# Turning normalised tokens with VectorE block transposes and SBUF-to-SBUF DMAs in a four-layer hybrid kernel

## The chip, the core and the metric

The kernel runs on one core of one Trainium2 chip. The time is device microseconds of one execution; the median of three runs of the kernel before is 2016.64 us.

## What is computed

The input x is 8 sequences of 1024 tokens with 256 features, float32. Four layers follow each other, each with a layernorm (no scale, no shift) in front and a residual around it:

```
x = x + softmax_attention(layernorm(x))   # 2 heads of 128, causal, half of each head rotated
x = x + feed_forward(layernorm(x))        # 768 hidden: (silu(x wg) * (x wu)) wd, integer weights / 127
x = x + linear_attention(layernorm(x))    # 8 heads of 64, elu+1 features, per-head decay, tanh gate
x = x + feed_forward(layernorm(x))        # the same weights again
```

The matrices multiply float32 values as a high part and a low part (`F32R`), in two to four matmuls each.

## The kernel before, in words

X, all 8192 tokens, stays in SBUF for the whole kernel: 64 tiles of 128 tokens by 256 features. The work goes in units of 512 tokens (UT = 4 tiles): 16 units per layer. Every projection needs the normalised tokens the other way round, features on the partitions, so each unit passes through the same steps, always for the unit or batch that comes next:

- VectorE (DVE) takes statistics (L121) and aggregates (L129), GpSimd (POOL) takes the reciprocal root (L153, L156), DVE normalises into `ln_xn` (L141).
- `SplitTransposed.pe` (L181 to L188) turns the unit on TensorE (PE): 8 transposes of 128x128 (4 tiles, 2 feature groups) into two PSUM banks.
- `act` (L192) copies the 128x1024 result out of PSUM as the high part, on ScalarE (ACT).
- `dve` (L196) subtracts it from the PSUM copy and writes the low part. `pe_wait` lets PE go on to the projections.

Each engine has its own list of instructions, written out by hand and run in order; semaphores (`Signal`) tie them together. An instruction that waits holds back everything behind it on its engine.

**Softmax attention** (`attention_phase`, L243): a turn per batch of 1024 tokens. First 8 query/key projections and the value projections, then 16 steps n (token tile i = n // 2, head n % 2), each with scores, row maximum, exponential, transposed probabilities, weighted values and output projection. In step 4 and 6 DVE takes the statistics of the next batch, in 9 and 11 it normalises, and in steps 14 and 15 PE, ACT and DVE turn and split the two halves. SP loads X in a loop (L333), one batch behind another, all before 52 us. POOL adds the rotated parts.

**Feed-forward** (`feed_forward_phase`, L722): a turn per unit, six iterations f. PE's order in each is gate(f), up(f), down(f-2); ACT's is silu(f), high part of h(f-1) (L818, L811); DVE's is h(f) (L865), low part of h(f-1) (L845), and at f = 1 the residual of the unit before (L852). Statistics are at f = 0 and 2, the normalisation at 3, PE's transposes at 4 (after up, before down), ACT's copy at the end of 4, DVE's subtraction at the start of 5. The parts have two sets of buffers, for even and odd units. SP only stores the output in the second feed-forward (L781).

**Linear attention** (`linear_attention_phase`, L955): a turn per batch, two halves of 512 tokens. 16 projections with their activations, then four chunks c: scores, outputs, state, keys; the gated output goes through a high part on ACT (`gated_high`) and a low part on POOL (`gated_low`). Statistics lie among the projections, the normalisation before chunk 0 (L1266), the transposes and the split in chunk 3 (L1422, L1147, L1273). The parts have one set of buffers.

## Time and profile before

| | |
|---|---|
| runs | 2016.64 us median, 2015.66 to 2017.07 |
| the profiled execution | span of 2018.8 us from the first to the last instruction, the one time there is for it |
| granted TensorE clock | 0.990 of 2.4 GHz over the span |
| PE / DVE / ACT / POOL busy | 1942.5 / 1340.9 / 890.8 / 335.7 us |
| softmax attention, feed-forward, linear attention, feed-forward | about 0 to 566, 569 to 858, 873 to 1720, 1726 to 2019 us |

Busy time is the sum of an engine's instructions; PE's matmuls overlap, and their ends are modelled, so starts are read rather than ends. A wait is shown in square brackets: the idle time before an instruction and what ended it. A line number is that of the kernel before; `SPq` and `ACTq` are the engines' queues issuing DMAs.

### The profile page before, as it was taken

What the parts mean: (1) busy time and instruction counts of PE and PEld (TensorE: products, weight loads), DVE (VectorE), ACT (ScalarE), POOL (GpSimd) and SP (SyncE); (2) the same over time, 40 slices, a digit from 0 to 9 for tenths busy, and PEclk for the clock granted to TensorE, in tenths of its full rate; (3) what the DMA queues carried; (4) which work ended last, traced back from release to release, by engine and by line L of the source; (5) the groups of instructions that cost most, each with busy time, mean ns of one, the idle gap of its engine ahead of it and who ended that gap; (6) DMA issues with size and microseconds to landing.
All of it is one profiled execution on the core that took longest, in us unless ns stands there. A gap on an engine that the chain in (4) does not pass through costs nothing. (4 is left out here: it accounts for less than half of the span.)

```text
span 2018.8 us, 36941 instructions
## 1 busy us (share of the span) xinstructions
PE 1942.5 (96%) x12803; PEld 1678.0 (83%) x12803; DVE 1340.9 (66%) x3222; ACT 890.8 (44%) x1708; POOL 335.7 (17%) x314
## 2 busy tenths in 40 slices
PE   6999999999899999979999999999999999999998
PEld 5888888888688888858888888888888888788887
DVE  5666566656557777756666666666666666677776
ACT  4556555655554444453333333333333333444443
POOL 2112211221100000032222222221222112000000
PEclk9999999999999999989999999999999999899999
DMA  6100000000010000010000000000000000000000
GB/s 221 48 1 0 0 0 0 0 0 0 1 53 0 0 0 0 0 52 1 2 1 1 0 0 0 0 0 0 0 0 0 0 1 1 11 32 31 31 29 34
DMA packets 21983, 27.91 MB, mean 14 GB/s; under 512 B 1057, under 2 KB 20129, under 8 KB 21537
## 3 DMA queue, kind: packets, MB, share of 16 engines
q1 hardware_dynamic: 20800, 24.32, 3.6%
q10 hardware_dynamic: 1120, 2.75, 0.4%
q8 instruction: 39, 0.64, 0.1%
q14 instruction: 24, 0.19, 0.0%
HBM read 18.69 MB, written 8.39 MB: 13 GB/s over the span
## 5 line engine op out<-in xcount | busy, mean ns | idle before, releaser
L818 ACT ACTIVATE ff_silu<-PS 128x512 f32<-128x512 f32 x192 | 115.3, 600 | 290.1 <-PE PS L903 290.1
L865 DVE SCALAR_TENSOR_TENSOR ff_h<-PS,ff_silu 128x512 f32<-128x512 f32 x192 | 132.8, 692 | 125.0 <-PE PS L903 114.0
L1119 ACT ACTIVATE lin_yg_hi<-stage 128x512 fp32r<-128x512 f32 x64 | 40.4, 632 | 384.9 <-DVE stage L1234 373.3
L914 PE MATMUL PS<-ff_w_hi,ff_h_hi 128*128 128x256 f32 x768 | 193.7, 285 | 1.0 <-ACT ff_h_hi L811 1.0
L914 PE MATMUL PS<-ff_w_hi,ff_h_lo 128*128 128x256 f32 x768 | 191.9, 282 | 0.0
L1084 POOL TENSOR_TENSOR lin_yg_lo<-stage,lin_yg_hi 128x512 fp32r<-128x512 f32 x64 | 81.9, 1280 | 577.6 <-ACT lin_yg_hi L1119 577.6
L1196 DVE TENSOR_TENSOR lin_AD<-PS,lin_decay 128x512 f32<-128x512 f32 x128 | 82.1, 682 | 131.5 <-PE PS L1342 131.5
L227 PE MATMUL PS<-ln_xh,lin_w_hi 128*128 128x512 f32 x384 | 152.4, 397 | 15.0 <-DVE lin_w_lo L1165 15.0
L903 PE MATMUL PS<-ln_xh,ff_w_hi 128*128 128x512 f32 x384 | 153.9, 401 | 5.1 <-ACT ff_w_hi L806 2.7
L633 PE MATMUL PS<-probT,v_a 128*128 128x128 f32 x1152 | 154.0, 279 | 4.1 <-DVE oT_lo L495 4.1
L633 PEld LDWEIGHTS PS<-probT,v_a 128*128 128x128 f32 x1152 | 138.9, 192 | 19.3 <-issue 12.7
L914 PEld LDWEIGHTS PS<-ff_w_hi,ff_h_hi 128*128 128x128 f32 x768 | 145.6, 190 | 10.8 <-ACT ff_h_hi L811 1.4
L903 PE MATMUL PS<-ln_xl,ff_w_hi 128*128 128x512 f32 x384 | 153.8, 401 | 0.0
L227 PE MATMUL PS<-ln_xl,lin_w_hi 128*128 128x512 f32 x384 | 151.0, 393 | 0.0
L227 PE MATMUL PS<-ln_xh,lin_w_lo 128*128 128x512 f32 x384 | 150.9, 393 | 0.0
L903 PE MATMUL PS<-ff_odd_xl,ff_w_hi 128*128 128x512 f32 x384 | 150.8, 393 | 0.0
L903 PE MATMUL PS<-ff_odd_xh,ff_w_hi 128*128 128x512 f32 x384 | 150.4, 392 | 0.0
L914 PEld LDWEIGHTS PS<-ff_w_hi,ff_h_lo 128*128 128x128 f32 x768 | 146.3, 190 | 4.9
L605 PE MATMUL PS<-qk 128*128 128x512 f32 (+3 forms) x384 | 144.7, 488 | 0.0
L500 DVE TENSOR_REDUCE neg_max<-PS 128x1 f32<-128x256 f32 (+7 forms) x128 | 96.6, 755 | 67.2 <-PE PS L608 65.6
L1355 PE MATMUL PS<-lin_v,lin_AD 128*128 128x65 f32 x1024 | 133.3, 273 | 0.0
L153 POOL TENSOR_SCALAR ln_var_eps<-ln_mean_var 128x4 f32<-128x4 f32 (+1 forms) x56 | 13.0, 231 | 718.3 <-DVE ln_mean_var L129 718.3
(156 smaller groups left out, 4934.2 us busy)
## 6 DMA issues: line engine op xcount, KB each, us to landing
X<-in_x SPq DMA_DIRECT2D x8, 1024.0 KB, 5.3
out_x<-X SPq DMA_DIRECT2D x16, 512.0 KB, 2.9
stage<-in_w_lin SPq DMA_DIRECT2D x1, 2048.0 KB, 7.6
stage<-in_w_gate SPq DMA_DIRECT2D x2, 768.0 KB, 4.3
stage<-in_w_up SPq DMA_DIRECT2D x2, 768.0 KB, 5.8
stage<-in_w_down SPq DMA_DIRECT2D x2, 768.0 KB, 8.1
cos<-in_cos ACTq DMA_DIRECT2D x1, 1024.0 KB, 8.3
qk<-in_w_qkv ACTq DMA_DIRECT2D x1, 768.0 KB, 7.2
```

What stands on the lines that cost most here:

```text
L227: last = nc.tensor.matmul(out, w, x, start=n == 0, stop=n == len(terms) - 1)
L500: nc.vector.tensor_reduce(neg_max[:, n:n + 1], score_rows(n), AX.X, ALU.max, negate=True).then_inc(max_done.sem, 1)
L605: last = nc.tensor.matmul(bank[:, 0:w], qk[:, 0, h, i * P:(i + 1) * P], qk[:, 1, h, c:c + w], start=True, stop=not diag)
L633: last = nc.tensor.matmul(O, V[:, j, h * DA:(h + 1) * DA], probT[:, n % 2, j, :], start=j == 0, stop=j == i)
L818: nc.scalar.activation(silu[:, f % 2, :], PS[:, 2 + f % 2, :], ACT.Silu, scale=W_SCALE).then_inc(silu_done.sem, 1)
L865: nc.vector.scalar_tensor_tensor(h[:, f % 2, :], PS[:, 4 + f % 2, :], W_SCALE, silu[:, f % 2, :], ALU.mult, ALU.mult).then_inc(h_done.sem, 1)
L903: ins = nc.tensor.matmul(PS[:, bank, :], w, x, start=n == 0, stop=n == len(parts) - 1)
L914: ins = nc.tensor.matmul(Y[:, t // 2, (t % 2) * M:(t % 2 + 1) * M], a[:, f % NH, t * P:(t + 1) * P], w[:, f % NF, :], start=f == 0 and n = ...
L1084: nc.gpsimd.tensor_tensor(yg_lo[:], yg, yg_hi[:].bitcast(F32), ALU.subtract).then_inc(yg_lo_done.sem, 1)
L1119: nc.scalar.activation(yg_hi[:], yg, ACT.Copy).then_inc(yg_hi_done.sem, 1)
L1196: nc.vector.tensor_tensor(AD[:, c % 2, r], PS[:, r, :].rearrange("p (j t) -> p j t", t=P), D[:].rearrange("p (j r) t -> p r j t", r=2)[:, ...
L1355: last = nc.tensor.matmul(bank[:, hh * VA:(hh + 1) * VA], AD[:, ch % 2, hh % 2, 2 * g + hh // 2, :], v[:, c, HG * g + hh, :], start=hh == ...
```

## The change

The transposes on PE go, in all four layers, and `SplitTransposed` with them. A unit is now turned so:

- DVE writes the normalised tokens with their features in four groups of 32, so that each group's columns of a unit stand together (`by_feature_group`).
- DVE transposes every 32x32 block of the unit in one instruction (`dve_blocks`).
- SP moves the blocks to their places with 16 DMAs inside SBUF, for each of four row groups and four column groups: 32 partitions by 8 pieces of 32 floats, 32 KB (`sp_move`). They land in the buffer of the low part.
- ACT copies that buffer as the high part (`act_high`), POOL subtracts it in place (`pool_low`). Neither touches PSUM.

In the softmax attention the block buffer is `swapped`, so SP waits until the values of the batch are projected, and the statistics, normalisations and blocks stand at steps 2, 4, 6 to 9 and ACT's copies at 11 and 13; SP loads batch 0 and 1 first and batch b + 2 in turn b. In the feed-forwards the statistics are taken a unit earlier, at f = 4 and 5, the normalisation is at f = 0, the blocks at f = 1, ACT's copy ahead of silu(4). In the linear attention SP waits for the half's last projection, and ACT's copy comes before the first `gated_high`. In the second feed-forward each store stands on SP behind the moves of a unit.

```diff
+SQ = 32
+NQ = P // SQ
+MOVES = NQ * NQ
+def by_feature_group(buf, t):
+    return buf.rearrange("p t m -> p (t m)").rearrange("p (c k t b) -> p c k t b", c=NQ, k=KT, t=UT)[:, :, :, t, :]
...
-            last = nc.vector.tensor_scalar(self.out[:, t, :], self.X[:, bass.ds(turn * self.tiles + t, 1), :],
-                                           self.mean_var[:, t, 0:1], self.rstd[:, t:t + 1],
+            out = by_feature_group(self.out[:, t // UT * UT:(t // UT + 1) * UT, :], t % UT)
+            x = self.X[:, bass.ds(turn * self.tiles + t, 1), :].rearrange("p a (k c b) -> p c (a k) b", k=KT, b=SQ)
+            last = nc.vector.tensor_scalar(out, x, self.mean_var[:, t, 0:1], self.rstd[:, t:t + 1],
...
+    def dve_blocks(self, dve, unit, before=None):
+        dve.wait_ge(self.ln.ready.sem, self.ln.ready.at(unit, self.unit + 1))
+        if before:
+            front, n = before
+            dve.wait_ge(front.landed.sem, front.landed.at(n, 16 * MOVES))
+        self.nc.vector.transpose(self.blocks.rearrange("p t m -> p (t m)"),
+                                 self.ln.out[:, self.unit * UT:(self.unit + 1) * UT, :].rearrange("p t m -> p (t m)")).then_inc(self.blocks_done.sem, 1)
+    def sp_move(self, sp, unit, par):
+        wait_alone(sp, self.blocks_done.sem, self.blocks_done.at(unit, 1), self.sp_passed)
+        lo = self.parts[par][1][:].bitcast(F32)
+        for r in range(NQ):
+            for c in range(NQ):
+                src = self.blocks[r * SQ:(r + 1) * SQ, c, :].rearrange("p (n b) -> p n b", b=SQ)
+                dst = lo[c * SQ:(c + 1) * SQ].rearrange("p k (t r b) -> p (k t) r b", t=UT, r=NQ)[:, :, r, :]
+                sp.dma_start(dst, src).then_inc(self.landed.sem, 16)
+    def act_high(self, act, unit, par):
+        hi, lo = self.parts[par]
+        act.wait_ge(self.landed.sem, self.landed.at(unit, 16 * MOVES))
+        self.nc.scalar.activation(hi[:], lo[:].bitcast(F32), ACT.Copy).then_inc(self.hi_done.sem, 1)
+    def pool_low(self, pool, unit, par):
+        hi, lo = self.parts[par]
+        pool.wait_ge(self.hi_done.sem, self.hi_done.at(unit, 1))
+        self.nc.gpsimd.tensor_tensor(lo[:], lo[:].bitcast(F32), hi[:].bitcast(F32),
+                                     ALU.subtract).then_inc(self.lo_done.sem, 1)
...
+        odd = sb("a1_xh", [P, KT, UN], F32R), sb("a1_xl", [P, KT, UN], F32R)
+        turned = [Turned(nc, ctx, f"a{half}", ln, swapped[:, 2 * half:2 * half + 2, :].rearrange("p s (z m) -> p (s z) m", m=M),
+                         env["norm"].parts if half == 0 else odd, half) for half in range(NHALF)]
+        sx = [t.pair(0) for t in turned]
...
+                def load_x(b):
+                    at = bass.ds(b * TB, TB)
+                    sp.dma_start(X[:, at, :], x_v[:, at, :]).then_inc(x_loaded, 16)
+                load_x(0)
+                for t in turned:
+                    t.sp_open(sp)
+                following.sp_open(sp)
                 sp.wait_ge(w_loaded, 16)
-                sp.wait_ge(x_loaded, 16)
-                with sp.Fori(0, NB - 1) as p:
-                    at = bass.ds((p + 1) * TB, TB)
-                    sp.dma_start(X[:, at, :], x_v[:, at, :]).then_inc(x_loaded, 16)
-                    wait_alone(sp, x_loaded, (p + 2) * 16, passed)
-
+                for t in turned:
+                    t.sp_move(sp, 0, 0)
+                load_x(1)
+                def turn(b, more):
+                    if more:
+                        wait_alone(sp, x_loaded, b * 16 + 32, passed)
+                        load_x(b + 2)
+                    wait_alone(sp, v_ready.sem, v_ready.at(b, TB), passed)
+                    for t in turned:
+                        t.sp_move(sp, b + 1, 0)
+                with sp.Fori(0, NB - 2) as b:
+                    turn(b, True)
                 load_ff_weights(sp, env, io)
+                turn(NB - 2, False)
+                sp.wait_ge(v_ready.sem, v_ready.at(NB - 1, TB))
+                following.sp_move(sp, 0, 0)
...
-                        if n >= NS - NHALF and not last:
-                            sx[n - (NS - NHALF)].act(act, b + 1)
-                        if n == NS - 2 and last and following:
-                            following.sx.act(act, 0)
+                        if n in (11, 13) and not last:
+                            turned[(n - 11) // 2].act_high(act, b + 1, 0)
+                        if n == NS - 3 and last:
+                            following.act_high(act, 0, 0)
...
-                        elif not last:
-                            sx[n + 2 - NS].dve(dve, b + 1)
-                        elif n + 2 == NS and following:
-                            following.sx.dve(dve, 0)
...
-                            if n in (4, 6):
+                            if n in (2, 4):
                                 dve.wait_ge(x_loaded, (b + 2) * 16)
-                                ln.dve_tile_stats(dve, b + 1, range(0, UT) if n == 4 else range(UT, TB))
-                            if n == 6:
+                                ln.dve_tile_stats(dve, b + 1, range(0, UT) if n == 2 else range(UT, TB))
+                            if n == 4:
                                 ln.dve_aggregate(dve, b + 1)
-                            if n in (9, 11):
-                                ln.dve_normalise(dve, b + 1, range(0, UT) if n == 9 else range(UT, TB))
-                        if n == 7 and last and following:
+                            if n in (6, 8):
+                                ln.dve_normalise(dve, b + 1, range(0, UT) if n == 6 else range(UT, TB))
+                            if n in (7, 9):
+                                if n == 7:
+                                    dve.wait_ge(rotated.sem, rotated.at(b, 2 * NHALF))
+                                turned[(n - 7) // 2].dve_blocks(dve, b + 1)
+                        if n == 6 and last:
                             following.ln.dve_normalise(dve, 0)
+                        if n == 7 and last:
+                            following.dve_blocks(dve, 0)
...
-                        if n + 2 >= NS and not last:
-                            sx[n + 2 - NS].pe(pe, b + 1, b + 1)
-                        if n + 2 == NS and last and following:
-                            following.sx.pe(pe, 0, 0)
...
+                def unit(u, par, first, left):
+                    upcoming = next_of(u, par, left)
+                    if upcoming:
+                        nfront, nu, npar = upcoming
+                        if not first:
+                            wait_alone(sp, up_ready.sem, up_ready.at(u - 1, NF), front.sp_passed)
+                        nfront.sp_move(sp, nu, npar)
+                    if following and first:
+                        sp.wait_ge(prep_lo, NPART)
+                        load_lin_weights(sp, env, io)
+                    if not following and not first:
+                        store(u - 1)
+                def store(u):
+                    wait_alone(sp, x_done.sem, x_done.at(u, 1), front.sp_passed)
+                    at = bass.ds(u * UT, UT)
+                    sp.dma_start(out_v[:, at, :], X[:, at, :]).then_inc(stored, 16)
...
+                def unit(u, par, first, left):
+                    upcoming = next_of(u, par, left)
+                    if upcoming:
+                        nfront, nu, npar = upcoming
+                        nfront.pool_low(pool, nu, npar)
+                    after = after_next(u, left)
+                    if after:
+                        after[0].pool_rstd(pool, after[1])
...
+                        if f == NF - 2 and upcoming:
+                            nfront, nu, npar = upcoming
+                            nfront.act_high(act, nu, npar)
                         act.wait_ge(gate_ready.sem, gate_ready.at(u, f + 1))
                         act.wait_ge(h_done.sem, h_done.at(u, f - 1))
                         nc.scalar.activation(silu[:, f % 2, :], PS[:, 2 + f % 2, :], ACT.Silu,
                                              scale=W_SCALE).then_inc(silu_done.sem, 1)
                         if f > 0 or not first:
                             high_part(u, f - 1)
-                        if f == NF - 2 and upcoming:
-                            _, _, nsx, nturn = upcoming
-                            nsx.act(act, nturn)
...
-                        if f == NF - 1 and upcoming:
-                            nsx.dve(dve, nturn)
...
-                        if f == 3 and upcoming:
-                            nln.dve_normalise(dve, nln_turn)
...
-                            if f == 0:
-                                nln.dve_tile_stats(dve, nln_turn, range(0, UT // 2))
-                            if f == 2:
-                                nln.dve_tile_stats(dve, nln_turn, range(UT // 2, UT))
-                                nln.dve_aggregate(dve, nln_turn)
-                    if last:
+                        if upcoming and f == 0:
+                            upcoming[0].ln.dve_normalise(dve, upcoming[1])
+                        if upcoming and f == 1:
+                            upcoming[0].dve_blocks(dve, upcoming[1], (front, u))
+                        if after and f == NF - 2:
+                            after[0].dve_tile_stats(dve, after[1], range(UT))
+                        if after and f == NF - 1:
+                            after[0].dve_aggregate(dve, after[1])
...
-                            if f == NF - 2 and upcoming:
-                                _, nln_turn, nsx, nturn = upcoming
-                                nsx.pe(pe, nturn, nln_turn)
...
+                def turn(b, first, last):
+                    for half in range(NHALF):
+                        nfront, n = next_of(b, half, last)
+                        wait_alone(sp, proj_ready.sem, proj_ready.at(b, NITEM * (half + 1)), front.sp_passed)
+                        nfront.sp_move(sp, n, 0)
...
+                            if c == 0:
+                                nfront.pool_low(pool, n, 0)
...
+                            if c == 0:
+                                nfront, n = next_of(b, half, last)
+                                nfront.act_high(act, n, 0)
...
+                        nfront.dve_blocks(dve, nturn, (front, b * NHALF + half))
...
-                            elif upcoming:
-                                pe.wait_ge(ad_done.sem, ad_done.at(b, 2 * ch + 2))
-                                upcoming[1].pe(pe, upcoming[2], upcoming[2])
```

## Rows read from the trace of the kernel before

**Rows 1.** The page: span, busy time of the engines, and DMA queue q1.
```profile
span 2018.8 us, 36941 instructions
...
PE 1942.5 (96%) x12803; PEld 1678.0 (83%) x12803; DVE 1340.9 (66%) x3222; ACT 890.8 (44%) x1708; POOL 335.7 (17%) x314
...
q1 hardware_dynamic: 20800, 24.32, 3.6%
```

**Rows 2.** Busy time by stage: the softmax attention from 20 to 566 us (window, its length, busy us).
```profile
20.00:566.00 546.00, 528.44 (x3513) 443.13 (x3513) 335.92 (x807) 320.07 (x789) 100.61 (x81) 1.00 0.05 15
```

**Rows 3.** Groups of instructions: name, count, busy us, mean ns of one, idle before and releaser.
```profile
L186 PE MATMUL PS<-ident,ln_xn 128*128 128x128 f32 x512 | 69.7, 281 | 14.1 <-DVE ln_xn L141 14.1
...
L192 ACT ACTIVATE ln_xh<-PS 128x1024 fp32r<-128x1024 f32 x40 | 41.2, 1029 | 18.5 <-PE PS L186 18.5
...
L196 DVE TENSOR_TENSOR ln_xl<-PS,ln_xh 128x1024 fp32r<-128x1024 f32 x40 | 49.0, 1225 | 37.6 <-ACT ln_xh L192 37.6
...
L1079 POOL TENSOR_TENSOR lin_w_o_lo<-stage,lin_w_o_hi 128x1024 fp32r<-128x1024 f32 x1 | 2.4, 2352 | 0.0
...
L156 POOL TENSOR_TENSOR ln_rstd<-ln_var_eps,ln_minus_half 128x4 f32<-128x4 f32 (+1 forms) x56 | 63.2, 1128 | 4.7
```

**Rows 4.** Timeline of DVE in one feed-forward unit (start, length in us): h(0) twice.
```profile
702.17 0.69 DVE L865 SCALAR_TENSOR_TENSOR ff_h<-PS,ff_silu 128x512 f32<-128x512 f32 x1 [0.38 <-PE PS L903]
...
719.99 0.69 DVE L865 SCALAR_TENSOR_TENSOR ff_h<-PS,ff_silu 128x512 f32<-128x512 f32 x1 [0.38 <-PE PS L903]
```

**Rows 5.** SP's DMA issues in order of time, and the time from issue to landing of one.
```profile
860.58 0.34 SPq L1040 DMA_DIRECT2D lin_bias<-in_b_g  x1
...
860.97 1.30 SPq L1041 DMA_DIRECT2D lin_decay_in<-in_decay  x1
...
862.32 0.43 SPq L1042 DMA_DIRECT2D lin_AD<-in_dist  x1
...
862.78 0.43 SPq L1043 DMA_DIRECT2D lin_rev<-in_rev  x1
...
lin_AD<-in_dist SPq DMA_DIRECT2D x1, 192.0 KB, 2.4
```

**Rows 6.** Timeline of DVE and ACT in the same feed-forward unit.
```profile
703.38 0.74 DVE L121 BATCH_NORM_STATS2 ln_stats<-X 128x6 f32 x2
...
704.05 0.60 ACT L818 ACTIVATE ff_silu<-PS 128x512 f32<-128x512 f32 x1 [1.68 <-PE PS L903]
```

**Rows 7.** PE's first matmul of the feed-forward, and two windows (the number before DMA's is PEclk).
```profile
568.81 0.77 PE L903 MATMUL PS<-ln_xh,ff_w_hi 128*128 128x512 f32 x1 [2.42 <-issue]
...
568.10:574.90 6.80, 6.09 (x14) 4.79 (x15) 1.18 (x3) 6.08 (x7) 0.00 (x0) 0.50 0.32 92
...
1726.50:1732.00 5.50, 5.48 (x13) 4.34 (x14) 5.50 (x5) 4.39 (x4) 0.00 (x0) 0.50 0.00 0
```

**Rows 8.** Timeline of one half of the linear attention: ACT, DVE, PE.
```profile
1226.72 0.63 ACT L1119 ACTIVATE lin_yg_hi<-stage 128x512 fp32r<-128x512 f32 x1 [11.50 <-DVE stage L1234]
...
1215.70 1.29 DVE L1196 TENSOR_TENSOR lin_AD<-PS,lin_decay 128x512 f32<-128x512 f32 x2 [3.98 <-PE PS L1342]
...
1232.79 1.04 PE L186 MATMUL PS<-ident,ln_xn 128*128 128x128 f32 x8
...
1233.66 1.00 PE L1355 MATMUL PS<-lin_v,lin_AD 128*128 128x65 f32 x8
```

**Rows 9.** Timeline of one batch of the softmax attention: steps 7, 11 and 13.
```profile
258.06 0.47 DVE L513 SCALAR_TENSOR_TENSOR X<-PS,row_inv,X 128x256 f32 x1
...
271.25 0.28 ACT L418 ACTIVATE oT_hi<-PS 128x128 fp32r<-128x128 f32 x1 [1.94 <-PE PS L633]
...
280.06 0.28 ACT L418 ACTIVATE oT_hi<-PS 128x128 fp32r<-128x128 f32 x1 [2.27 <-PE PS L633]
```

**Rows 10.** The kernel's first normalisation and first projection.
```profile
12.61 2.67 DVE L141 TENSOR_SCALAR ln_xn<-X,ln_mean_var,ln_rstd 128x256 f32<-128x256 f32 x8 [2.31 <-POOL ln_rstd L156]
...
19.17 0.77 PE L227 MATMUL PS<-ln_xh,wqkv_hi 128*128 128x512 f32 x1 [1.39 <-DVE ln_xl L196]
```

More of the change, by code:

```diff
@@ L175, in act_open @@
     def act_open(self, act):
         open_signals(act, self.hi_done)
-    def dve_open(self, dve):
-        open_signals(dve, self.lo_done)
-    def pe(self, pe, turn, ln_turn):
-        ln = self.ln
-        pe.wait_ge(ln.ready.sem, ln.ready.at(ln_turn, self.unit + 1))
-        for t in range(UT):
-            for k in range(KT):
-                last = self.nc.tensor.transpose(self.psum[:, k, t * P:(t + 1) * P],
-                                                ln.out[:, self.unit * UT + t, k * P:(k + 1) * P], self.ident[:])
-        last.then_inc(self.transposed.sem, 1)
@@ new lines, in pe_wait, with pair, __init__, pool_open @@
+    def pe_wait(self, pe, unit):
+        pe.wait_ge(self.hi_done.sem, self.hi_done.at(unit, 1))
+        pe.wait_ge(self.lo_done.sem, self.lo_done.at(unit, 1))
+    def pair(self, par):
+        return Pair(*self.parts[par])
+class Front(Turned):
+    def __init__(self, nc, ctx, name, env):
+        super().__init__(nc, ctx, name, Layernorm(nc, ctx, f"{name}_ln", UT, env["X"], env["norm"]),
+                         env["norm"].xn[:, UT:TB, :], env["norm"].parts)
+    def dve_open(self, dve):
+        self.ln.dve_open(dve)
+        super().dve_open(dve)
+    def pool_open(self, pool):
+        self.ln.pool_open(pool)
+        super().pool_open(pool)
@@ L264, in attention_phase @@
         ln = Layernorm(nc, ctx, "a_ln", TB, X, env["norm"])
-        sx = [SplitTransposed(nc, ctx, f"a{half}", PS[:, 2 * half:2 * half + 2, :], ident, ln, half,
-                              parts=env["norm"].parts if half == 0 else None)
-              for half in range(NHALF)]
         qk = sb("qk", [P, 2, HA, T])
@@ L516, in turn @@
                 def turn(b, first, last):
-                    if last and following:
+                    if last:
                         following.ln.dve_stats(dve, 0)
@@ L920, in units, with unit @@
                 def units(terms):
-                    def unit(u, par, turn, first, last):
-                        sx[par].pe_wait(pe, turn)
-                        upcoming = next_of(u, par, turn, last)
+                    def unit(u, par, first, left):
+                        front.pe_wait(pe, u)
                         for f in range(NF):
@@ L941, in unit @@
                                 down(u, f - LAG, terms)
-                        if last:
+                        if not left:
                             for f in range(NF - LAG, NF):
```

201 lines of the change are left out of this document (87 added, 114 removed).

## The prediction

> **What bounds the kernel now.** I read the page's busy line first, then the busy time by stage, then one unit of each stage instruction by instruction. TensorE is busy 96% of the span and the next engine, VectorE, 66% [rows 1]. A single stage looks the same: TensorE is busy 528.4 of the softmax attention's 546 us [rows 2]. So whatever leaves TensorE's queue is worth its full time, as long as nothing else comes late. The 512 transposes of normalised tokens (8 for each of 64 units of 512 tokens) are such work [rows 3]. What they cost in place is read from starts, since ends overlap: in the linear attention the eight take 0.87 (1232.79 to 1233.66) [rows 8]. A feed-forward unit takes 17.82 us from one h(0) to the next (702.17 to 719.99) [rows 4]; less the transposes and a hand-over of 0.1 that leaves 16.8, six iterations of 2.8.
>
> **What is removed and added.** Removed per unit: 8 PE transposes, a 1.03 us ACT copy out of PSUM, a 1.22 us DVE subtraction [rows 3]. Added per unit: one DVE block transpose of 128x1024, 16 DMAs of 32 KB on SP's one queue, an ACT copy and a POOL subtraction of 128x1024. No row shows a DVE transpose of float32; the nearest is the subtraction of the same size, 1.22 us [rows 3]. I take 1.2; as low as 1.1 or twice as much cannot be excluded. POOL's 128x1024 subtraction took 2.35 [rows 3]. ACT and DVE are thus even. What is new is the latency of the moves, X, from the block transpose's end to the last landing.
>
> **X.** Four issues that stand back to back on SP start 0.39, 1.35 and 0.46 apart [rows 5]. I take 0.50, near the two that agree; the ends are 0.39 and the mean of the three, 0.73. The load among them lands 2.4 after its issue [rows 5]. X = 0.1 for SP to wake + 15 x 0.50 + 2.4 = 10.0 us. Beside this, each DMA engine moves 16 pieces of 128 bytes per DMA. Over the page's queue q1, 20,800 packets took 3.6% of 16 x 2018.8 us, 56 ns each at 1.17 KB [rows 1]; scaled by bytes that is 6 ns. So a DMA lasts between 0.1 and 0.9 us on the engines. I take a value under 0.5 (an eighth of the bytes), so that the issue sets the pace; 0.9 is kept for a rival.
>
> **Feed-forward, where X is not covered.** In unit u, DVE normalises unit u+1 at iteration 0 and turns blocks at iteration 1; ACT takes the high part at iteration 4, ahead of silu(4), so everything behind it on ACT waits: silu(4), the high part of h(3), then down(3) on PE. Unstalled, from PE's start of the unit: h(0) at 2.1, then the list of the loop below puts the end of the blocks at 8.4; down(3) is due at 5 x 2.8 + 1.84 = 15.8. Down(3) needs, after landing, 1.0 + 0.5 + 0.6 on ACT and 0.6 on DVE plus hand-overs, 2.9 us. X could be 4.5 at most. It is 10.0. So every unit stalls, and the unit becomes a loop. From the landing T, with start-to-start times: high part 1.0 [rows 3] and silu 0.55 [rows 6] and hand-overs bring h(4) to T+1.6. Then DVE has h and low 1.2 a pair (702.17 to 703.38), four statistics 1.45 [rows 4, 6]: h(4), low(3), statistics, h(5), low(4), and an aggregate of 0.55 end at T+6.05. POOL's rstd takes 1.13 [rows 3] after an addition of about 0.2, with hand-overs: T+7.5. Normalise 1.3, h(1) and low(0) 1.2, residual 1.15 (the size of the subtraction in rows 3), blocks 1.2: T+12.4. Plus X: 22.4 us a unit at full clock, against 17.82.
>
> **The clock in that loop.** PE resumes at T+2.9 and ends up(5) about 5 us before: one idle stretch of 5 us a unit. In the trace the granted clock fell from 1.00 to 0.50 (2.4 to 1.2 GHz) at 568.1, within an idle of 2.4 us that ended at 568.8; after work resumed it stayed at 0.50 for 6.1 us there and 5.5 us in the last stage [rows 7]. I take the fall for likely in each unit, with 5.8 us at half. PE's work from the resume to up(1)'s end is two iterations of 2.8, 5.6 us at full clock; with 5.8 us at half it takes 8.5, so up(1) ends at T+11.4. Then h(1), low(0), residual, blocks 3.6: T+15.0; plus X = 25.0 us. It happens in 31 units (16 in the first feed-forward, the last of them for the linear attention's tokens; 15 in the second): 31 x (25.0 - 17.8) = +223 us. The Trainium skill ("TensorE: Matmul & The Clock Gate", Part 1) has an idle TensorE fall to half rate and rise after sustained work; by that rule a unit is 25.0, without it 22.4, and the fall at 568.1 [rows 7] agrees with it.
>
> **Linear attention.** SP waits for the last of 16 projections, because the parts are overwritten. ACT has that one copied at 1226.72 - 11.50 = 1215.2, so it was ready at 1214.5. Landed 1224.5, high part to 1225.5; ACT's next instruction starts at 1226.72 after its wait of 11.5 for VectorE [rows 8]: covered, with 1.2 to spare. The blocks fall into a DVE idle of 3.98 us before 1215.70 [rows 8]: free. POOL only has the gated low parts then, 6 us apart; 2.35 fits. If that cover went (X over 11.2), each extra us would delay the gated high part. Gain 16 x 0.87 = -14.
>
> **Softmax attention.** TensorE is the bound [rows 2]. The blocks of step 7 follow the residual of 258.06; as that step loses what moves to step 4, I put their end at 259.1, the landing at 269.1. ACT's slot for the first high part is the idle of 1.94 before 271.25, for the second the 2.27 before 280.06: from 269.3 and 277.8 [rows 9]. The second half's 16 issues queue behind the first's: 259.2 + 31 x 0.50 + 2.4 = 277.1. Both covered, barely. Statistics moved to steps 2 and 4 meet a busier DVE; I charge 0.25 a batch. Gain: 2 x 0.87 - 0.25 = 1.5 a batch, -12 in all. **Start-up:** nothing covers the first move. Normalised at 12.61 + 2.67; blocks 16.4, landed 26.4, high 27.4, low (2.35, rows 3) 29.8; the first projection stood at 19.17 [rows 10]: +10.7. The input load of a batch is issued a whole batch (546 / 8 = 68 us) before its statistics: nothing. In the second feed-forward the 16 stores stand behind the moves on SP; nobody waits for them but the end, where only the last one is open as before: nothing.
>
> **Sum.** +223 + 10.7 - 14 - 12 = +208 on a span of 2018.8, the one time of the profiled execution; the median of the three runs is 2.2 lower. 2016.6 + 208 = 2225 us.
>
> **Rivals.**
> A, the forecast (0.60): own range 2170 to 2300, from issue 0.42 to 0.62 and a DVE transpose of up to 2.4 (+1.2 a unit).
> B, the same stall without the fall of the clock (0.20): 31 x 4.6 = +143, less 15: 2144. For it: only one idle of this kind is in the rows, and it was at the end of a thinner stretch of work.
> C, the engines or the descriptor writing are the pace, up to 0.9 us a DMA (0.13): X = 16, unit 31.0, +409; in the softmax attention the second landing comes at 290 instead of 277, +10 a batch; in the linear one landing 1230.7, +4 a unit: about 2550. At 0.65 a DMA the unit is 27.25, +293, and the total about 2310. Against it: 128 bytes is an eighth of the packets in the rows.
> D, faster (0.05): the moves are covered also in the feed-forward. It decides at X = 4.5, that is at 0.14 us an issue; then 31 x -1.0 - 14 - 12 + 5 = -52: 1965. Against it: no issue in rows 5 takes under 0.34. The Trainium skill ("DMA: Bandwidth & Descriptors", "Anatomy of one DMA", written for GpSimd's path) puts a sequencer's dispatch at about 50 ns. By it X would be 3.2 and the transfer hidden; the 0.39 and more between issues [rows 5] speak against it for this queue.
> E, gains and losses cancel (0.02).
> That the transposes stay on PE somewhere is not possible by the diff: all of L186 is gone.
>
> **Range and chances.** Range 2120 to 2330: it holds A, B and the near part of C. A measurement of this kernel can tell about 0.2% (4 us) from no change. Slower 0.93 (A, B, C), same 0.02, faster 0.05.
>
> **What would show it.** Right: feed-forward units of 24 to 26 us; ACT before the high part waiting for a DMA some 5 us a unit, PE before down(3) idle 5 us a unit; granted clock near 0.8 there; SP's issues 0.5 apart, 1024 of them; attention stages shorter by 12 and 14 us but for a later first matmul near 30 us. Wrong: issue intervals under 0.2, or landings long after the last issue, or a wait for the DMA in the attention stages.

## The result, and the profile after

| | before | after |
|---|---|---|
| median, four runs each on the same chip | 2016.86 us (2015.66 to 2017.27) | 2319.86 us (2310.70 to 2321.08) |
| ratio | | 1.149, 95% interval 1.1469 to 1.151 |
| profiled span | 2018.8 us | 2317.5 us |
| granted clock over the span | 0.990 | 0.923 |

The kernel became 303 us slower; 2225 were forecast, in a range of 2120 to 2330. The page of the kernel after, beside [rows 1, 3]: the busy lines, the clock in 40 slices, queue q1, the chain that ended last, four groups and three kinds of DMA issue.

```profile
span 2317.5 us, 37114 instructions
...
PE 1943.6 (84%) x12291; PEld 1676.5 (72%) x12291; DVE 1361.1 (59%) x3222; ACT 885.4 (38%) x1708; POOL 489.0 (21%) x378
...
PEclk9999999999978778878999999999999988888878
...
q1 hardware_dynamic: 299328, 57.94, 12.3%
...
SPq L214 6%; PE PS L984 4%; PE PS L995 3%; DVE ff_h_lo L933 1%; ACT ff_silu L909 1%; DVE ln_xn L203 1%; DMA ff_odd_xl<-ln_xn 1%; DMA ln_xl<-ln_xn 1%; DVE ff_h L949 0%; ACT ff_w_hi L894 0%; DVE X L940 0%; DVE ln_xn L153 0%; DVEq L948 0%; DVE
...
L995 PE MATMUL PS<-ff_w_hi,ff_h_hi 128*128 128x256 f32 x768 | 217.5, 310 | 269.0 <-DVE ff_h_lo L933 266.2
...
L949 DVE SCALAR_TENSOR_TENSOR ff_h<-PS,ff_silu 128x512 f32<-128x512 f32 x192 | 130.9, 682 | 432.7 <-ACT ff_silu L909 319.2
...
L219 ACT ACTIVATE ln_xh<-ln_xl 128x1024 fp32r<-128x1024 f32 x40 | 42.3, 1058 | 356.4 <-DMA ln_xl<-ln_xn 330.0
...
L933 DVE TENSOR_TENSOR ff_h_lo<-ff_h,ff_h_hi 128x512 fp32r<-128x512 f32 x192 | 164.9, 859 | 0.2
...
ln_xl<-ln_xn SPq DMA_DIRECT2D x512, 32.0 KB, 2.0
...
ff_odd_xl<-ln_xn SPq DMA_DIRECT2D x256, 32.0 KB, 2.0
...
ln_xl<-swapped SPq DMA_DIRECT2D x128, 32.0 KB, 2.0
```

PE is as busy as before, 1943.6 us, in a span 299 us longer: it has 512 transposes less to do, and does part of the rest at half clock. DVE is busy for 20 us more and POOL for 153 us more, but both stay below PE; what grew is waits. SP was not on the chain before; now its issues of the moves (L214) are the first line of it, with 6% of the span. The clock line is low in just two stretches, the two feed-forwards. ACT's high part waits 330.0 us for landings in one buffer alone. The low part of h has a mean of 859 ns; before it was 682 ns, with the same 192 instructions.

**Where the 299 us of the two spans lie.** I split both at the same instructions: first and last exponential of the softmax attention, first and last silu of each feed-forward, first and last decayed scores of the linear attention. Two of the rows that this rests on (count, min/median/max ns, first and last start):

```profile
L909 ACT ACTIVATE ff_silu<-PS x96: 578/597/600, 596.4 to 1028.1; 128x512 f32<-128x512 f32 x96
...
L1280 DVE TENSOR_TENSOR lin_AD<-PS,lin_decay x128: 680/681/692, 1071.2 to 1857.3; 128x512 f32<-128x512 f32 x128
```

| stretch | before | after | change | forecast |
|---|---|---|---|---|
| start to the first exponential | 36.4 | 51.6 | +15.2 | +10.7 |
| softmax attention, first to last exponential | 518.7 | 528.1 | +9.4 | -12 |
| first feed-forward, first to last silu | 280.2 | 431.7 | +151.5 | |
| linear attention, first to last decayed scores | 807.6 | 786.1 | -21.5 | -14 |
| second feed-forward | 279.1 | 424.2 | +145.1 | |
| both feed-forwards | 559.3 | 855.9 | +296.6 | +223 |
| the three crossings and the tail (17.9, 40.1, 29.4, 9.4 before) | 96.8 | 95.8 | -1.0 | 0 |

So the feed-forwards hold nearly all of it, as forecast, and 74 us more than forecast: 9.6 us a unit over 31 units, where 7.2 were expected. The other 17 us that the forecast of the span lacked are 21 in the softmax attention and 4.5 at the start, less 7.5 in the linear attention and 1 in the crossings.

**One feed-forward unit**, beside [rows 4, 6]: the timeline of ACT, POOL, DVE, PE and SP in order of time.

```profile
807.62 1.06 ACT L219 ACTIVATE ln_xh<-ln_xl 128x1024 fp32r<-128x1024 f32 x1 [9.65 <-DMA ln_xl<-ln_xn]
...
808.75 2.35 POOL L224 TENSOR_TENSOR ln_xl<-ln_xl,ln_xh 128x1024 fp32r<-128x1024 f32 x1 [20.13 <-ACT ln_xh L219]
...
809.25 0.69 DVE L949 SCALAR_TENSOR_TENSOR ff_h<-PS,ff_silu 128x512 f32<-128x512 f32 x1 [10.19 <-ACT ff_silu L909]
...
809.85 1.79 DVE L933 TENSOR_TENSOR ff_h_lo<-ff_h,ff_h_hi 128x512 fp32r<-128x512 f32 x1
...
811.79 0.55 PE L995 MATMUL PS<-ff_w_hi,ff_h_hi 128*128 128x256 f32 x1 [8.48 <-DVE ff_h_lo L933]
...
819.29 0.28 PE L995 MATMUL PS<-ff_w_hi,ff_h_hi 128*128 128x256 f32 x1
...
821.83 1.24 DVE L203 STREAM_TRANSPOSE ln_xn<-ln_xn 128x1024 f32<-128x1024 f32 x1
...
823.17 10.46 SPq L214 DMA_DIRECT2D ff_odd_xl<-ln_xn  x16
...
835.00 1.06 ACT L219 ACTIVATE ff_odd_xh<-ff_odd_xl 128x1024 fp32r<-128x1024 f32 x1 [9.71 <-DMA ff_odd_xl<-ln_xn]
...
836.63 0.69 DVE L949 SCALAR_TENSOR_TENSOR ff_h<-PS,ff_silu 128x512 f32<-128x512 f32 x1 [10.25 <-ACT ff_silu L909]
```

From h(4) to the next h(4) it is 836.63 - 809.25 = 27.38 us, against 17.82 before. The blocks end at 823.07, the last piece has landed at about 834.9: X = 11.9. The 16 issues take 10.46, 0.65 each. ACT idles 9.71 behind the landing, PE 8.48 behind ACT and DVE. From the landing at about 807.5 to PE's resume (811.79) it is 4.3 us, and from there to the end of up(1), which down(5) of the unit before follows at 819.29, 7.5. The windows of the same unit (length, then PE, PEld, DVE, ACT, POOL busy, PEclk, DMA share, GB/s):

```profile
807.00:811.70 4.70, 0.00 (x0) 0.00 (x0) 2.45 (x3) 3.06 (x5) 2.35 (x1) 0.50 0.03 5
...
811.70:815.90 4.20, 4.11 (x14) 3.65 (x15) 2.74 (x10) 0.24 (x1) 1.18 (x2) 0.51 0.00 0
815.90:823.00 7.10, 7.10 (x44) 6.22 (x43) 6.09 (x11) 3.11 (x6) 0.09 (x1) 1.00 0.00 0
```

The granted clock is 0.50 in the last 4.7 us of PE's idle. After it PE works 4.2 us at 0.51, then at full speed. Over the first feed-forward the granted clock is 0.81, over the second 0.82.

### The profile page after: what moved, and what is told of

It reads as the page before. It is cut to its first block and busy times, and to the rows that moved or that the text cites. A ratio compares the mean times of both kernels' runs of the same rounds, so it can differ in the third digit from the quotient of the medians.

```text
span 2317.5 us, 37114 instructions
## 1 busy us (share of the span) xinstructions
PE 1943.6 (84%) x12291; PEld 1676.5 (72%) x12291; DVE 1361.1 (59%) x3222; ACT 885.4 (38%) x1708; POOL 489.0 (21%) x378
## 3 DMA queue, kind: packets, MB, share of 16 engines
q1 hardware_dynamic: 299328, 57.94, 12.3%
## 5 line engine op out<-in xcount | busy, mean ns | idle before, releaser
L995 PE MATMUL PS<-ff_w_hi,ff_h_hi 128*128 128x256 f32 x768 | 217.5, 310 | 269.0 <-DVE ff_h_lo L933 266.2
L995 PEld LDWEIGHTS PS<-ff_w_hi,ff_h_hi 128*128 128x128 f32 x768 | 163.2, 212 | 291.7 <-issue 281.4
L995 PE MATMUL PS<-ff_w_hi,ff_h_lo 128*128 128x256 f32 x768 | 213.6, 305 | 0.0
L224 POOL TENSOR_TENSOR ln_xl<-ln_xl,ln_xh 128x1024 fp32r<-128x1024 f32 x40 | 94.5, 2363 | 484.3 <-ACT ln_xh L219 484.3
L219 ACT ACTIVATE ln_xh<-ln_xl 128x1024 fp32r<-128x1024 f32 x40 | 42.3, 1058 | 356.4 <-DMA ln_xl<-ln_xn 330.0
L995 PEld LDWEIGHTS PS<-ff_w_hi,ff_h_lo 128*128 128x128 f32 x768 | 164.7, 214 | 5.1
L984 PE MATMUL PS<-ln_xh,ff_w_hi 128*128 128x512 f32 x384 | 161.5, 420 | 6.1 <-ACT ff_w_hi L894 2.6
L933 DVE TENSOR_TENSOR ff_h_lo<-ff_h,ff_h_hi 128x512 fp32r<-128x512 f32 x192 | 164.9, 859 | 0.2
L984 PE MATMUL PS<-ff_odd_xh,ff_w_hi 128*128 128x512 f32 x384 | 161.7, 421 | 0.0
L984 PE MATMUL PS<-ff_odd_xl,ff_w_hi 128*128 128x512 f32 x384 | 159.6, 416 | 0.0
```

The source lines that it names most:

```text
L224: self.nc.gpsimd.tensor_tensor(lo[:], lo[:].bitcast(F32), hi[:].bitcast(F32), ALU.subtract).then_inc(self.lo_done.sem, 1)
L933: nc.vector.tensor_tensor(h_lo[:, f % NH, :], h[:, f % 2, :], h_hi[:, f % NH, :].bitcast(F32), ALU.subtract).then_inc(lo_done.sem, 1)
L984: ins = nc.tensor.matmul(PS[:, bank, :], w, x, start=n == 0, stop=n == len(parts) - 1)
L995: ins = nc.tensor.matmul(Y[:, t // 2, (t % 2) * M:(t % 2 + 1) * M], a[:, f % NH, t * P:(t + 1) * P], w[:, f % NF, :], start=f == 0 and n = ...
```

## Experiments

Four questions stood open: whether the price of a move lies in its issue or in what it carries, what the clock adds, why the low part of h(3) is slow, and whether the moves or only their place do the harm. The line numbers of these kernels differ a little from those of the kernel after. The kernel before was run again beside the experiments and took 2016.3 to 2018.3 us; the ratios are to those runs.

### Half the DMAs, or half of each DMA

The diff is that of half the DMAs; for half of each DMA the second line has `NQ, UT * KT // 2`.

```diff
+        if name != "lin":
+            self.rows, self.pieces = NQ // 2, UT * KT
...
-        for r in range(NQ):
+        for r in range(self.rows):
...
-                sp.dma_start(dst, src).then_inc(self.landed.sem, 16)
+                sp.dma_start(dst[:, 0:self.pieces], src[:, 0:self.pieces]).then_inc(self.landed.sem, 16)
```

> Part of the computation is left out: in the feed-forwards only two of the four row groups are moved, 8 DMAs of 32 KB a unit instead of 16, so half of the normalised tokens there are stale. The changed kernel takes 2320 us, and a feed-forward unit 27.4. Theory (the moves stand on the path, and their number times 0.65 us sets the latency): 8 x 0.65 = 5.2 us less from the blocks' end to the last landing, 6.7 instead of 11.9; unit 22.2; in 30 units -156, so 2164. If TensorE's idle time gets so short that its clock no longer falls, up to 2 us a unit less again: 2104. Rival (the moves are hidden, something else holds the unit at 27): no change, 2320.

> Part of the computation is left out: in the feed-forwards each of the 16 DMAs of a unit moves four of its eight pieces of 128 bytes, so half of the normalised tokens there are stale. Same bytes and pieces as eight whole DMAs, twice the number of DMAs. Theory 1 (an issue has a fixed price on the queue, 0.65 us, whatever it carries): unit stays at 27.4, total 2320. Theory 2 (the pieces set the pace, by descriptors written or by the engines that move them: 256 a DMA): issues 0.33 apart, 5.2 us less a unit, total 2164 as with half the DMAs. Between the two if an issue has a part of each.

Both kernels move the same half of the bytes. With half the DMAs: 2147.74 us, ratio 1.0652 (1.0613 to 1.0691), between the 2164 and the 2104 of the theory. With half of each DMA: 2316.05 us, ratio 1.1482 (1.1463 to 1.1501), as slow as the changed kernel and as theory 1 has it. SP's issues and the landing in the kernel with half of each DMA:

```profile
823.02 10.31 SPq L215 DMA_DIRECT2D ff_odd_xl<-ln_xn  x16
```
```profile
ff_odd_xl<-ln_xn SPq DMA_DIRECT2D x256, 16.0 KB, 1.8
```

An issue costs 0.64 us with 128 pieces and 0.65 with 256. The time from issue to landing falls from 2.0 to 1.8. So the price is paid per issue, and neither the pieces nor the bytes set the pace. While SP issues, the 16 DMA engines are busy for 28% of the time in the changed kernel and for 15% with half of each DMA, at the same pace. The kernel with half the DMAs also shows what the clock costs, without having been made for it. PE's resume in three neighbouring units, DVE's h(4) in four, and the half-clock stretches of the first two units:

```profile
787.53 0.55 PE L999 MATMUL PS<-ff_w_hi,ff_h_hi 128*128 128x256 f32 x1 [3.26 <-DVE ff_h_lo L937]
...
810.37 0.55 PE L999 MATMUL PS<-ff_w_hi,ff_h_hi 128*128 128x256 f32 x1 [3.27 <-DVE ff_h_lo L937]
...
832.12 0.36 PE L999 MATMUL PS<-ff_w_hi,ff_h_hi 128*128 128x256 f32 x1 [3.26 <-DVE ff_h_lo L937]
```
```profile
784.98 0.69 DVE L953 SCALAR_TENSOR_TENSOR ff_h<-PS,ff_silu 128x512 f32<-128x512 f32 x1 [4.97 <-ACT ff_silu L912]
...
807.82 0.69 DVE L953 SCALAR_TENSOR_TENSOR ff_h<-PS,ff_silu 128x512 f32<-128x512 f32 x1 [4.98 <-ACT ff_silu L912]
...
829.57 0.69 DVE L953 SCALAR_TENSOR_TENSOR ff_h<-PS,ff_silu 128x512 f32<-128x512 f32 x1 [4.96 <-ACT ff_silu L912]
...
849.85 0.69 DVE L953 SCALAR_TENSOR_TENSOR ff_h<-PS,ff_silu 128x512 f32<-128x512 f32 x1 [4.99 <-ACT ff_silu L912]
```
```profile
787.50:793.20 5.70, 5.67 (x18) 4.93 (x19) 2.76 (x11) 1.11 (x2) 1.26 (x2) 0.50 0.00 0
...
810.30:813.50 3.20, 3.13 (x12) 2.87 (x13) 2.72 (x10) 0.00 (x0) 0.23 (x1) 0.50 0.00 0
```

The idle before the resume is the same. In the first two units the matmul runs at half clock (0.55), in the third at full (0.36), and the units last 22.84, 21.75 and 20.28 us. So a fall costs by how long the half clock lasts after it: 2.6 us for 5.7 us of it, 1.5 us for 3.2.

### Two issuing queues

```diff
-                        nfront.sp_move(sp, nu, npar)
+                        nfront.sp_move(sp, nu, npar, range(NQ // 2))
...
+                        if f == 2 and upcoming:
+                            act.wait_ge(up_ready.sem, up_ready.at(u - 1, NF))
+                            upcoming[0].act_move(act, upcoming[1], upcoming[2])
```

> In the feed-forwards ScalarE's queue issues half of the 16 DMAs of a unit, beside SyncE's. Theory (the pace is that of one issuing queue): X falls from 11.9 to 8 x 0.65 + 2 = 7.3 us, unit 22.5 to 23.4 (ScalarE's eight issues of 0.65 can make silu(3) late by up to 0.5), total 2320 - 31 x 4.0 to 4.9 = 2170 to 2200. Rival (the 16 DMA engines or the descriptors are the pace, shared by both queues): issues on each queue 1.3 apart, X still near 12, and ScalarE blocked for 10 us: total 2320 or more.

Measured: 2120.53 us, ratio 1.0522 (1.0505 to 1.054). The two queues in one unit, and ACT's copy behind them:

```profile
809.54 5.48 SPq L221 DMA_DIRECT2D ff_odd_xl<-ln_xn  x8
...
809.47 5.26 ACTq L221 DMA_DIRECT2D ff_odd_xl<-ln_xn  x8
...
816.41 1.06 ACT L226 ACTIVATE ff_odd_xh<-ff_odd_xl 128x1024 fp32r<-128x1024 f32 x1 [0.39 <-DMA ff_odd_xl<-ln_xn]
```

Eight issues take 5.3 to 5.5 us on each queue, side by side; from the blocks' end to ACT's copy it is 7.0 us. The rival, a pace that both queues share, falls. The kernel is some 50 us faster than the theory's 2170. Its clock falls less often: the granted clock is 0.983 over the span, PE's idle before down(3) is 2.81 us in most units, and its first matmul after it runs at half clock in 4 of the 31 units (31 of 31 in the changed kernel). That this is where the 50 us come from is read, not tested: by the 1.5 to 2.6 us of a fall, 27 units without one would give 40 to 70. The Trainium skill ("DMA: Bandwidth & Descriptors", "Issuing engines are not separate DMA queues") says that starting DMAs from several engines saves only the sequencers' time, which it calls usually small beside the DMA itself. The rule agrees, but "usually small" does not hold here: that time was 10.46 of X's 11.9 us.

### GpSimd's subtraction nearly removed

```diff
-                        nfront.pool_low(pool, nu, npar)
+                        nfront.pool_low(pool, nu, npar, P)
```

> Part of the computation is left out: in the feed-forwards GpSimd subtracts only 128 of 1024 columns, so most of the low parts are wrong. In the changed kernel VectorE's low part of h(3) takes 1.79 us where the same instruction elsewhere takes 0.68, and GpSimd's subtraction of 2.35 us runs beside it. Theory (the two share access to SBUF, and the low part of h(3) is on the path between landing and next blocks): with the subtraction gone it takes 0.68, the unit loses 1.1 us, total 2320 - 31 x 1.1 = 2286. Rival (VectorE is slow there for another reason, its copy of h is written at that time by ScalarE): still 1.79, total 2320.

Measured: 2295.44 us, ratio 1.1389 (1.137 to 1.1408), 24 us less than the changed kernel; 34 had been expected. The low part of h has its mean back, and the instruction that had taken 1.79 takes 0.68:

```profile
L934 DVE TENSOR_TENSOR ff_h_lo<-ff_h,ff_h_hi 128x512 fp32r<-128x512 f32 x192 | 130.4, 679 | 0.2
```
```profile
829.99 0.68 DVE L934 TENSOR_TENSOR ff_h_lo<-ff_h,ff_h_hi 128x512 fp32r<-128x512 f32 x1
```

The units are 829.39 - 802.93 = 26.46 long, 0.9 less. So POOL's subtraction is what slows DVE's: in the changed kernel POOL's subtraction runs from 808.75 to 811.10, and DVE's, begun at 809.85, ends 0.5 us after it. DVE's h(4) at 809.25, with one input in PSUM, took its 0.69 beside the same subtraction. The Trainium skill ("SBUF — State Buffer", "SBUF: two separate sides") has VectorE instructions with two inputs in SBUF and GpSimd instructions that read SBUF exclude each other, the later one blocked to the end of the earlier. The trace agrees, for the blocked instruction and for the one that was not.

### Filling TensorE's idle

```diff
+                            if f == NF - 1 and left:
+                                for _ in range(32):
+                                    nc.tensor.matmul(PS[:, 0, :], gate_hi[:, 0, 0:P], sx[par].hi[:, 0, :], start=True, stop=True)
                             if f >= LAG or not first:
                                 down(u, f - LAG, terms)
```

> Added work, nothing left out: in 30 of the 31 feed-forward units that stall, TensorE does 32 matmuls of 512 columns whose results nobody reads before down(3), into a free PSUM bank, 32 x 0.23 = 7.4 us of its idle of 8.5. Theory (the idle lowers the granted clock, and the half clock after it is paid in the loop): clock 1.00 at down(3), and 1.5 us less a unit, as two neighbouring units of the run with half the DMAs differed (21.75 with the fall, 20.28 without): 2320 - 30 x 1.5 = 2275. Rival (what follows the stall is set by VectorE's list and the DMAs, the clock costs nothing): 2320, whatever the clock. The fillers end before the parts of h(3) are there, so they should delay nothing.

Measured: 2275.63 us, ratio 1.129 (1.1272 to 1.1308). PE around the resume of down(3), and its resume in the next unit:

```profile
736.91 7.41 PE L1019 MATMUL PS<-ff_odd_xh,ff_w_hi 128*128 128x512 f32 x32
745.62 0.36 PE L995 MATMUL PS<-ff_w_hi,ff_h_hi 128*128 128x256 f32 x1 [1.30 <-DVE ff_h_lo L933]
...
771.21 0.36 PE L995 MATMUL PS<-ff_w_hi,ff_h_hi 128*128 128x256 f32 x1 [1.33 <-DVE ff_h_lo L933]
```

A kernel with 960 matmuls more is 44 us faster. These two units are 25.59 us apart, where it was 27.38: 1.8 us less, for a half-clock stretch of some 4 us, between the two prices above. The mean over the 30 units is 1.5, because the first units of each feed-forward and a few later ones gain less; that it is the forecast's own 1.5 is in part luck. The rest of the loss stays, so the rival that the clock costs nothing falls, and so does any account by the clock alone. By the Trainium skill ("TensorE: Matmul & The Clock Gate", Part 1) an idle TensorE falls to half rate; the windows above and this run agree.

### The high parts of the softmax attention later

```diff
-                        if n in (11, 13) and not last:
-                            turned[(n - 11) // 2].act_high(act, b + 1, 0)
+                        if n in (12, 15) and not last:
+                            turned[(n - 12) // 3].act_high(act, b + 1, 0)
```

> The changed kernel, only ScalarE's two high-part copies of the softmax attention stand in steps 12 and 15 instead of 11 and 13. In the changed kernel ScalarE waits there 1.6 and 3.8 us a batch for landings, and TensorE 2.0 us behind it; two of seven batches are 2 us longer still, with the clock at 0.98. Theory (these stalls are why the batches are 67.7 to 69.6 us instead of 65.7): both waits vanish, 7 x 2.0 + 2 x 2 = -18: 2302. Rival (the copies then come late for the next batch's projections, since GpSimd needs 2.35 us after each): the wait moves to TensorE's batch start, 2320 or more.

Measured: 2298.02 us, ratio 1.1389 (1.1373 to 1.1406). In the changed kernel ACT's copy in step 13 and PE behind it:

```profile
235.07 1.06 ACT L219 ACTIVATE a_xh<-a_xl 128x1024 fp32r<-128x1024 f32 x1 [3.77 <-DMA a_xl<-swapped]
...
236.76 1.80 PE L694 MATMUL PS<-probT,v_a 128*128 128x128 f32 x14 [2.00 <-DVE oT_lo L558]
```

With the later copies this wait is gone, and a batch lasts 65.5 us (blocks at 202.8 and 268.3). From blocks to blocks it was 67.7 in three batches of the changed kernel and 69.3 to 70.3 in three others, with the granted clock at 0.98 there; before the change it was 67.2. The theory (2302) is met, its rival falls. From the first to the last exponential it is now 506.4 us, 12.3 less than in the kernel before.

### Two units ahead

`second_next` gives unit u + 2, or unit 0 of the following layer.

```diff
-                        if not first:
-                            wait_alone(sp, up_ready.sem, up_ready.at(u - 1, NF), front.sp_passed)
-                        nfront.sp_move(sp, nu, npar)
+                    if first:
+                        front.sp_move(sp, 1, 1)
+                    ahead = second_next(u, par, left)
+                    if ahead:
+                        wait_alone(sp, up_ready.sem, up_ready.at(u, NF), front.sp_passed)
+                        ahead[0].sp_move(sp, ahead[1], ahead[2])
...
+                        if ahead and f == 3:
+                            ahead[0].ln.dve_normalise(dve, ahead[1])
+                        if ahead and f == NF - 2:
+                            ahead[0].dve_blocks(dve, ahead[1], (front, u + 1))
```

> The same turning, but in the feed-forwards unit u + 2 instead of u + 1 is prepared during unit u: statistics at f = 1, aggregate at 2, normalisation at 3, blocks at 4; SyncE issues the moves when up(5) of unit u is through. Landing about 15.8 + 11.9 = 27.7 us after the unit's start, that is 10.9 us into unit u + 1 of 16.8 us, ScalarE's copy at iteration 4 of it (11.2), GpSimd's low part by 15. Theory (the loss was uncovered latency alone): no stall but one of about 9.5 us in the first unit of each feed-forward; units of 16.8; feed-forward stages 280 and 279 us become about 275 each. The attentions stay as in the changed kernel (+23 with the start-up, -21 with what surrounds it): total 2017 - 11 + 2 = 2008. Rival 1 (VectorE, ScalarE and GpSimd with their contention for SBUF cannot hold 16.8): 17.8 or more a unit, total 2038 or more. Rival 2 (the moves as such disturb others): a feed-forward unit stays over 20.

Measured: 2023.86 us, ratio 1.0034 (1.0021 to 1.0046): 296 us of the 303 are back, though every move is still made. ACT's copies in two units, and one unit as a window:

```profile
756.92 1.06 ACT L219 ACTIVATE ff_odd_xh<-ff_odd_xl 128x1024 fp32r<-128x1024 f32 x1 [1.24 <-DMA ff_odd_xl<-ln_xn]
...
774.04 1.06 ACT L219 ACTIVATE ln_xh<-ln_xl 128x1024 fp32r<-128x1024 f32 x1 [1.22 <-DMA ln_xl<-ln_xn]
```
```profile
740.00:757.14 17.14, 17.01 (x97) 14.62 (x96) 13.87 (x27) 7.64 (x14) 3.67 (x3) 1.00 0.19 31
```

PE is busy 17.01 of 17.14 us. A unit is 0.7 shorter than the 17.82 before, not 1.0, and a stage (first to last silu, 281.1 and 282.3 us) no shorter than before (280.2 and 279.1). Both rivals fall, since a unit is neither 17.8 nor over 20. 2008 was missed by 16; 13 of them are the two stages, for which 275 each had been expected.

### The softmax attention of before, and the first unit on TensorE

The hybrid kernel has the deep version's feed-forwards and linear attention, and `attention_phase` with `SplitTransposed` of the kernel before; unit 0 of the first feed-forward is turned on PE too.

> As the deep version, but the softmax attention (and the first unit of the first feed-forward) is that of the kernel before, transposes on TensorE. Theory (in the softmax attention the turning loses, +23 us from start-up and stalls; in the linear one it gains 21): the first silu of the feed-forward at 573 again instead of 596; total 2008 - 23 = 1985, faster than the kernel before by 1.6%. Rival (part of the 23 us comes back later, or the linear gain needs the softmax attention's change): 2000 to 2017.

Measured: 2001.89 us, ratio 0.9925 (0.9912 to 0.9938), 0.7% faster than the kernel before. 1985 was missed by 17, 16 of which the deep version had missed already; the step from it is 22.0 us, where 23 were expected. The total lies in the rival's range, but neither of its reasons holds. The first silu is back at 571.9, and the linear attention keeps its gain, 786.3 us from its first to its last decayed scores:

```profile
L1324 DVE TENSOR_TENSOR lin_AD<-PS,lin_decay x128: 679/681/692, 896.9 to 1683.2; 128x512 f32<-128x512 f32 x128
```

But the feed-forward stages take 283.1 and 281.6 us. At 17.14 a unit, 15.8 units would be 271. The suspect is the move for unit 1, which nothing covers. In the last kernel PE turns unit 1 of each feed-forward too, against the hybrid kernel:

```diff
-                    if first:
-                        front.sp_move(sp, 1, 1)
...
+                        if first and f == 3:
+                            first_split.dve(dve, 1)
...
-                        if first and f == 1:
-                            front.dve_blocks(dve, 1, (front, 0))
...
+                            if first and f == 2:
+                                first_split.pe(pe, nth_in_split, 1)
```

> As the hybrid, but unit 1 of each feed-forward, whose turning nothing can hide, is turned on TensorE as in the kernel before (normalised at f = 0, transposes at f = 2, low part at the start of f = 3). In the deep version a unit takes 17.14 us once the pipeline is full, yet a feed-forward stage (first to last silu, 15.8 units) still takes 281 to 283 us instead of 271. Theory (the difference is the one uncovered move in its first unit): stages of 272 to 273, total 2002 - 10 - 10 = 1982, 1.7% faster than the kernel before. Rival (the stages lose it elsewhere, in the second unit or the last): 2002 stays.

Measured: 1978.31 us (1976.98 to 1980.43), ratio 0.9807 (0.9794 to 0.9821): 1.9% faster than the kernel before, with its whole interval below 1, and the fastest kernel of this study. Its silus in the first and the second feed-forward:

```profile
L951 ACT ACTIVATE ff_silu<-PS x96: 575/600/602, 569.7 to 841.9; 128x512 f32<-128x512 f32 x96
...
L951 ACT ACTIVATE ff_silu<-PS x96: 572/600/603, 1694.9 to 1967.3; 128x512 f32<-128x512 f32 x96
```

272.2 and 272.4 us. One uncovered move had cost 9 to 11 us in each feed-forward, 20 of the 24 us between the two kernels, and the rival falls.

## Why the prediction was right, and where its sizes were off

The direction, the place and the mechanism came out as forecast. The size did so only just: +303 us for +208, 10 us below the upper end of the range and outside the 2170 to 2300 of its own rival A. The range held because it also took in the near part of rival C. Of the signs named, "ACT before the high part waiting" and "PE before down(3) idle" were seen at 9.7 and 8.5 us where 5 were expected, and the clock was near 0.8; but the unit was 27.38, not 24 to 26, and one sign of being wrong, "a wait for the DMA in the attention stages", was there.

- **Mechanism: right.** X was not covered in the feed-forward, ACT's high part held silu(4), and the unit became a loop of landing, work and X. The deep version shows that the place of the moves did it: the same moves two units ahead leave a unit of 17.14.
- **X: mis-sized.** "I take 0.50" for the interval between issues; it measured 0.65. The landing took 2.0, not 2.4. X was 11.9 instead of 10.0, 1.9 us a unit, 59 of the 74 us missing in the feed-forwards. Rival A's own end, 0.62, was too low as well. The mean of the three intervals of [rows 5], 0.73, kept as an end, was nearer than the value that was taken, which had set the 1.35 among them aside.
- **The loop: 15.5 for 15.0, the other 15 of the 74 us.** Two terms are off and partly cancel. PE resumed 4.3 us after the landing, not 2.9: 1.1 of it is DVE's low part of h(3), which took 1.79 beside POOL's subtraction and was charged 0.6. That POOL does not slow DVE was put at nothing, without a reason. From the resume to the end of up(1) it was 7.5 us, not 8.5: the half clock lasted 4.2 us, not the 5.8 read from [rows 7]. The price itself was right: 2.6 us were charged for 5.8 us of it, and 5.7 us cost 2.6 in the kernel with half the DMAs; in this loop a fall cost 1.5 to 1.8.
- **Rival B** (no fall of the clock, 2144) is refuted: down(3)'s first matmul took 0.55 in all 31 such units of the trace, and filling the idle gave 44 us.
- **Rival C** had the number but not the cause. It priced 0.65 a DMA at 27.25 us a unit and about 2310 in total; 27.38 and 2320 came out. But it put the pace down to the engines or to the writing of descriptors. Halving the pieces changed nothing and a second queue cut X from 11.9 to 7.0, so the pace is that of one issuing queue, the forecast's own mechanism.
- **Rival D** put the turning point at X = 4.5. With eight DMAs X was 6.6 (820.07 + 1.24 to 827.94) and the unit still stalled, which fits; that point itself was not reached.
- **Linear attention: right in kind, mis-sized.** -21.5 instead of -14, and ACT's copy there waits for a landing and not for DVE (X had grown past the 11.2 of the forecast), with 4.8 us of waiting for DVE still behind it: covered. PE's busy time between the first and last decayed scores fell from 796.0 to 776.7 us. The rows show 0.87 us for the eight transposes themselves; the first transposed output of the next unit used to start 0.2 to 0.3 us late as well (1240.25 to 1240.77, where 0.23 is usual), in all 15 places, and after the change it starts 0.23 behind in all. Both together are some 17 us; the other 4 are open. That the removed subtraction on DVE made the gap is an idea, not tested.
- **Softmax attention: wrong.** "Both covered, barely" failed with X: with issues of 0.65 the second half's landing comes 22.4 us after the first half's blocks (212.6 to 235.0), where 18 were forecast. The first half's came late too: ACT waited 1.65 and 3.8 us a batch, PE 2.0, and half the batches ran at a clock of 0.98. That turned -12 into +9.4. With the copies one and two steps later the stage gained 12.3, the -12 of the forecast.
- **Start-up: mis-sized.** The first projection came at 31.81, forecast 29.9, by the 1.9 of X. The second half's 16 issues hold ACT until 39.8 before it copies rotated parts, so 12.6 us late at the first projection became 15.2 at the first exponential.

## What to carry to other kernels

A DMA inside SBUF cost its queue 0.65 us with 32 KB and 0.64 with 16; with 16 of them in a row the latency was some 12 us, and here it had to be laid over a whole unit of other work before it was free. Only then did taking work from the bounding engine pay: one unit ahead it lost 303 us; two units ahead it came out nearly even (ratio 1.0034); with the turnings that nothing covers left on TensorE, and the softmax attention as before, it won 40. Where a forecast says "covered, barely", its chance should be that of the interval it rests on, not of its middle.

## What the runs showed of the hardware

- SP's and ACT's queues issue such DMAs at 0.65 to 0.69 us each, side by side, without slowing one another noticeably; 128 or 256 pieces of 128 bytes in a DMA make a difference of 0.01 us to the issue and 0.2 us to the landing.
- All packets of q1 together took 12.3% of 16 x 2317.5 us for 299,328 packets, 15 ns each, where [rows 1] had 56 ns at six times the size; while SP issued, the engines were busy 28% of the time, far from being the limit.
- DVE's block transpose of 128x1024 float32 took 1.24 us, as a subtraction of that size does.
- A DVE subtraction with both inputs in SBUF waited for a POOL subtraction to end (1.79 for 0.68 us); DVE's h(4), with an input in PSUM, did not (0.69).
- After the same idle of 3.26 us the clock had fallen in two units and not in the next; the falls cost 2.6 us (half clock for 5.7 us) and 1.5 us (for 3.2), and a kernel with 7.4 us of useless matmuls in PE's idle was faster than one without.
